# The beginning of a transformer block on one core: zero matmuls, order of the condition rows, and weight splits rearranged

## What is computed

```
emb = silu(t) @ ada_w + ada_b                        # six rows of 512 for each of 4 batches
shift_msa, scale_msa, gate_msa, shift_mlp, scale_mlp, gate_mlp = split(emb, 6)
norm  = ln(x) * (1 + scale_msa) + shift_msa
h     = gelu(norm @ ssm_w1 + ssm_b1)
x     = x + gate_msa * (h @ ssm_w2 + ssm_b2)
norm2 = ln(x) * (1 + scale_mlp) + shift_mlp
hf    = gelu_tanh(norm2 @ ff_w1 + ff_b1)
x     = x + gate_mlp * (hf @ ff_w2 + ff_b2)
# second block: gamma * ln(x) + beta with gamma = w @ Wg.T + bg, beta = w @ Wb.T + bb,
# then qkv, softmax attention over 16 heads, projection, and the same style norm again
```

## Time and profile before

| | |
|---|---|
| median of 3 runs | 1886.05 us (1886.03 to 1886.64) |
| the profiled execution | 1888.92 us |
| its span in the profile | 1887.1 us |
| PE, DVE, ACT, POOL busy | 1817.0, 1249.5, 778.2, 1181.6 us |
| mean granted TensorE clock | 0.987 |

### The profile page before, as it was taken

One profiled execution on the slowest core, in us unless ns is written; L12 is line 12 of the kernel. 1 busy time (PEld: TensorE's weight loads), 2 busy tenths in 40 slices (PEclk: granted clock), 3 DMA queues, 4 the chain that ended last, 5 costly groups with the idle time before them and its releaser, 6 DMA issues. The chain is left out here.

```text
span 1887.1 us, 26913 instructions
## 1 busy us (share of the span) xinstructions
PE 1817.0 (96%) x9530; PEld 1215.4 (64%) x9530; DVE 1249.5 (66%) x2053; ACT 778.2 (41%) x1376; POOL 1181.6 (63%) x655
## 2 busy tenths in 40 slices
PE   7899999999998999999899999999999999999995
PEld 3588888888887788888555555545555554454584
DVE  4565555655655454546787777777777777787399
ACT  2223123222222222221476666666666666666200
POOL 2675465466454212111588888888898888898455
PEclk9999999999999999999899999999999999999998
DMA  7310110100103555474777778778787877765894
GB/s 249 128 41 23 56 34 22 56 33 22 56 1 134 184 188 191 156 244 142 188 164 174 179 182 183 175 171 187 177 183 175 184 175 177 172 150 138 261 400 145
DMA packets 131013, 278.46 MB, mean 148 GB/s; under 512 B 23846, under 2 KB 41382, under 8 KB 122840
## 3 DMA queue, kind: packets, MB, share of 16 engines
q1 hardware_dynamic: 98772, 191.71, 33.6%
q0 software_dynamic: 9264, 66.11, 17.2%
q10 hardware_dynamic: 22872, 19.28, 3.2%
HBM read 134.42 MB, written 75.80 MB: 111 GB/s over the span
## 5 line engine op out<-in xcount | busy, mean ns | idle before, releaser
L1558 DVE TENSOR_REDUCE at_mrow<-banks 128x1 f32<-128x512 f32 x976 | 593.7, 679 | 169.7 <-PE banks L1404 169.6
L1654 POOL TENSOR_TENSOR at_sums<-at_probs 128x2048 f32<-128x2048 f32 x127 | 599.0, 4716 | 94.5 <-DMA at_sums<-at_sums 80.6
L1538 ACT ACTIVATE at_probs<-banks 128x512 f32<-128x512 f32 x1024 | 519.0, 621 | 185.6 <-PE banks L1422 180.5
L1404 PE MATMUL banks<-early_ks,early_qs 96*128 96x512 f32 x976 | 406.7, 417 | 9.8 <-DVE at_mrow L1558 5.4
L1422 PE MATMUL banks<-early_qs,early_ks 98*128 98x512 f32 x1024 | 408.4, 418 | 2.3 <-ACT at_probs L1538 1.8
L1404 PEld LDWEIGHTS banks<-early_ks,early_qs 96*128 96x128 f32 x976 | 184.8, 189 | 141.8 <-DVE at_mrow L1558 87.7
L1422 PEld LDWEIGHTS banks<-early_qs,early_ks 98*128 98x128 f32 x1024 | 193.9, 190 | 107.8 <-ACT at_probs L1538 83.3
L1434 PE MATMUL banks<-at_probs,at_v 128*32 128x512 f32 x2048 | 250.4, 606 | 1.6 <-DMA at_v<-v_scratch 1.6
L71 PE MATMUL banks<-l_ht,l_weights 128*128 128x512 f32 x768 | 179.4, 393 | 7.0 <-ACT l_gt L657 7.0
L71 PE MATMUL banks<-qk_nt,l_weights 128*128 128x512 f32 x768 | 179.8, 392 | 3.0 <-ACT qk_gt L1039 3.0
L71 PE MATMUL banks<-l_weights,l_hf 128*128 128x512 f32 x768 | 177.3, 390 | 0.0
(11 more groups left out here) (143 smaller groups left out, 2100.6 us busy)
## 6 DMA issues: line engine op xcount, KB each, us to landing
at_sums<-at_sums POOLq DMA_DIRECT2D x63, 1024.0 KB, 8.3
qk_scratch<-qk_out SPq DMA_DIRECT2D x64, 512.0 KB, 2.8
early_ks<-qk_scratch SPq DMA_DIRECT2D x48, 512.0 KB, 4.9
early_qs<-qk_scratch SPq DMA_DIRECT2D x96, 256.0 KB, 5.6
attn_scratch<-at_out SPq DMA_DIRECT2D x32, 512.0 KB, 7.6
o_a<-attn_scratch SPq DMA_DIRECT2D x32, 512.0 KB, 12.9
chunk_in<-x SPq DMA_DIRECT2D x8, 1024.0 KB, 5.2
v_scratch<-qk_v ACTq DMA_DIRECT2D x32, 256.0 KB, 2.4
```

The source lines that it names most:

```text
L1404: pe.matmul(em[n % 3][:], qs[0:96, slot, half, j, c * P:(c + 1) * P], ks[0:96, slot, j, keys * CH:(keys + 1) * CH], start=True, stop=True) ...
L1538: nc.scalar.activation(probs[:, i % 4, j, :], et[n % 3][:], ACT.Exp).then_inc(exp_done, 1)
L1558: nc.vector.tensor_reduce(mrow[:, half, keys, u:u + 1], em[n % 3][:], AX.X, ALU.max).then_inc(max_done, 1)
L1654: nc.gpsimd.tensor_tensor(into, probs[:, a], probs[:, a + 1], ALU.add).then_inc(pair_ready, 1)
```

## The change

- In setup PE runs 12 matmuls on two zeroed tiles before its first row. DVE writes the ones into `ones2` only after them (`warmed`).
- PE multiplies the row `GATE_MSA` before it turns the first two rows, not after.
- The copy and the split of weight 1 leave setup: ACT and DVE do them at the start of step 0.
- ACT copies weights 2 and 3 after the second and third tile of L1, and 4 and 5 after the tiles of `U_T2`. DVE splits 2 and 3 between the L1 tiles and 4 after the tiles of `U_T1`; POOL splits 5 after all eight tiles of `U_F1`. PE waits for the last two before its loop, as it did.
- SP issues the loads of weights 2 and 3 ahead of the late rows.
- PE computes two late rows before `turn_ln2` and the third after it. DVE adds their biases in two parts and takes the statistics of the next chunk after the second tile of `U_T2`, not before the first.
- POOL takes the inverse deviation of the next chunk between the second and third of those tiles.

```diff
@@ setup_stage @@
-            act.wait_ge(raw_loaded[1], 16)
-            nc.scalar.copy(sh.w0[:, HI, 1, :], sh.w0_raw[:, LO, 1, :]).then_inc(w_hi, 1)
...
+            pe.wait_ge(dve_step, 2)
+            for _ in range(WARM):
+                ins = pe.matmul(ps[7][:], sh.ones2[:], sh.bias_rows[:], start=True, stop=True)
+            ins.then_inc(warmed, 1)
             pe.wait_ge(silu_ready, 1)
             row(SHIFT_MSA)
             row(SCALE_MSA)
+            row(GATE_MSA)
             pe.wait_ge(consts_loaded, 6 * 16)
             turn_rows(0, 2)
-            row(GATE_MSA)
...
             dve.wait_ge(dve_step, 2)
+            dve.wait_ge(warmed, 1)
             nc.vector.memset(sh.ones2[0:2].bitcast(F32), 1.0)
...
             take_turned(1)
-            low_weight(1)
...
-            pool.wait_ge(w_lo, 2)
+            pool.wait_ge(w_lo, 1)
@@ l0_stage, SP @@
             load_gate(0, 0)
+            for n in range(2, 4):
+                load_weight(n)
             load_late_rows()
-            for n in range(2, 6):
-
-                sp.dma_start(raw_weight(sh, weights, n), weights[n]).then_inc(ff_loaded[n - 2], 16)
+            for n in range(4, 6):
+                load_weight(n)
@@ l0_stage, PE @@
                 if first:
-                    late_rows()
+                    late_rows(range(2))
                     turn_ln2()
+                    late_rows(range(2, 3))
...
-                    pe.wait_ge(ff1_lo, 2)
+                    pe.wait_ge(ff1_lo, 3)
...
-            pe.wait_ge(ff2_lo, 2)
+            pe.wait_ge(ff1_lo, 4)
+            pe.wait_ge(ff2_lo, 1)
@@ l0_stage, ACT @@
+                def high_feed_forward(n):
+                    if n in (1, 2):
+                        high_weight(n + 1, ff_loaded[n - 1])
+
+                if first:
+                    high_weight(1, sh.w2_loaded)
+                gelu(ACT.Gelu, l1_done, s, U_L1, range(KT), C_B1, lo, high_feed_forward if first else None)
                 affine(1, s, (s, U_T2), b, hi)
+                if first:
+                    for n in range(4, 6):
+                        high_weight(n, ff_loaded[n - 2])
@@ l0_stage, DVE @@
+                if first:
+                    hi_parts(uses(s, U_T2), KT, ht, next_stats)
+                    add_late_bias(range(2, 3))
...
+                if first:
+                    dve.wait_ge(ff_hi, 4)
+                    split_in_place(nc.vector, sh, 4).then_inc(ff1_lo, 1)
                 hi_parts(uses(s, U_F1 - (KT if last else 0)), FT, hf)
@@ l0_stage, POOL @@
                 add_gated_bias(0, s, b, x)
-                if first:
-                    split_ff2(4)
...
-                if first:
-                    split_ff2(5)
-                if first:
                     lo_parts(uses(s, U_F1), KT, hf)
                     pool.wait_ge(late_stored, 16 * 4)
                     lo_parts(uses(s, U_F1) + KT, KT, hf[:, :, KT:])
+                    split_ff2(5)
```

More of the change, by code:

```diff
@@ L189, in setup_stage @@
         mod_w_loaded = [sem(f"su_mod_w_loaded{i}") for i in range(NROWS)]
-        raw_loaded = [sem(f"su_raw_loaded{i}") for i in range(2)]
+        raw_loaded = [sem("su_raw_loaded"), sh.w2_loaded]
         silu_ready = sem("su_silu_ready")
@@ L585, in step, with late_rows @@
                     to_features(w1, nt, KT, [m], [a[m]], l1_done)
+                if first:
+                    pe.wait_ge(ff1_lo, 1)
                 to_tokens(w2, ht, KT, b, uses(s, U_L1), l2_done)
-                def late_rows():
+                def late_rows(which):
                     pe.wait_ge(gt_full, uses(s, U_L1) + KT)
-                    for n, row in enumerate(LATE_ROWS):
+                    for n in which:
+                        row = LATE_ROWS[n]
                         pe.wait_ge(late_loaded, 16 * 8)
@@ L667, in gelu, with high_weight @@
                                          bias=sh.cols[:, col + m:col + m + 1]).then_inc(gt_full, 1)
+                    if behind is not None:
+                        behind(n)
             def step(s, parity, b, b_next, last):
                 lo, hi = banks(parity, 0), banks(parity, 1)
[L671 to L676, removed]
+                first = isinstance(s, int) and s == 0
+                def high_weight(n, loaded):
+                    act.wait_ge(loaded, 16)
+                    nc.scalar.copy(sh.w0[:, HI, n, :], sh.w0_raw[:, LO, n, :]).then_inc(ff_hi, 1)
+                def high_feed_forward(n):
[4 more added lines that the diff above has]
+                gelu(ACT.Gelu, l1_done, s, U_L1, range(KT), C_B1, lo, high_feed_forward if first else None)
                 affine(1, s, (s, U_T2), b, hi)
+                if first:
+                    for n in range(4, 6):
+                        high_weight(n, ff_loaded[n - 2])
                 if not last:
@@ L698, in hi_parts @@
                     nc.vector.tensor_copy(dst[:, HI, i, :], gt[:, i % 2, :]).then_inc(gt_hi, 1)
+                    if behind is not None:
+                        behind(i)
             def ln_stats(which, s, src):
@@ L745, in step, with add_late_bias, next_stats @@
                 ln_apply(1, s, x1[:, parity])
[L746 to L749, removed]
-                if first:
+                def add_late_bias(which):
                     dve.wait_ge(late_loaded, 16 * 8)
-                    for n in range(len(LATE_ROWS)):
+                    for n in which:
                         dve.wait_ge(late_ps_ready, n + 1)
                         nc.vector.tensor_tensor(rows[:, n], lo[n][0:B, :], rows[:, n], ALU.add).then_inc(late_ready, 1)
+                def next_stats(i):
+                    if i == 1:
+                        add_late_bias(range(2))
+                        dve.wait_ge(x_loaded, 16 * (s + 1))
+                        ln_stats(0, s + 1, x)
+                if first:
+                    hi_parts(uses(s, U_T2), KT, ht, next_stats)
+                    add_late_bias(range(2, 3))
+                else:
+                    if not last:
+                        dve.wait_ge(x_loaded, 16 * (s + 1))
+                        ln_stats(0, s + 1, x)
+                    hi_parts(uses(s, U_T2), KT, ht)
                 if not last:
@@ L828, in step @@
                 add_gated_bias(0, s, b, x)
[L829 to L831 removed]
+                if not first:
                     add_gated_bias(1, s - 1, b_prev, x1[:, 1 - parity])
                 inv_std(1, s)
[L834 removed]
+                if first:
+                    lo_parts(uses(s, U_T2), KT // 2, ht)
                     inv_std(0, s + 1)
[L836 removed]
+                    lo_parts(uses(s, U_T2) + KT // 2, KT // 2, ht[:, :, KT // 2:])
+                else:
+                    if not last:
+                        inv_std(0, s + 1)
+                    lo_parts(uses(s, U_T2), KT, ht)
                 if first:
```

27 lines of the change are left out of this document (17 added, 10 removed).

## The result

| | before | changed |
|---|---|---|
| median of 15 runs | 1886.64 us | 1892.98 us |
| lowest and highest | 1883.39, 1889.71 | 1888.53, 1897.75 |
| span of the profiled execution | 1887.1 us | 1890.2 us |
| its time | 1888.92 us | 1892.00 us |

The medians lie 6.3 us apart. The ratio of the two sets of runs is 1.0035, with a 95% interval of 1.0028 to 1.0043, which is 5.3 to 8.1 us slower. (More runs of the kernel before were made beside the changed one; the table ahead of the prediction has the first three.)

What follows compares the result with a forecast made beforehand. PE, busy in all but 4%, bounds the kernel, so L1 of chunk 1's start decides: 7.4 us later, plus 2.3 low clock, less a 0.6 wait, +9.0 on 1886.05 gives 1895.0 us; range 1888.5 to 1899.

Steps and rivals of the forecast that it cites:

- Setup: Before step 0: turning at 19.95 us, 2.1 later, yet the stage gives 1.9 and L1 starts at 33.65.
- L1 of step 0: First half of step 0: with no long wait ahead, L1 takes 11.04 us in place of 12.74.
- Weights 2 and 3: First half of step 0: loads without 3 MB ahead land at 43.5 and 46.1 us; L2 ends at 59.0.
- Engines that take turns: DVE splits and POOL tiles exclude each other at two places; without exclusion the sum is 2.4 us less.
- PE at the end of F1: Second half of step 0: PE done with F1 at 96.9 us, before 105.19, so 8.3 us won on PE.
- The low clock behind the new wait: L1 of chunk 1: low clock after PE's 15.7 us wait costs 2.3 us more, between 1.7 and 3.4.
- POOL's tail: POOL's work from the U_T1 tiles to the weight 5 split: 86.4 us plus 26.1, ending at 112.5; PE waits for it.
- The 0.6 ahead of L2: L2 of chunk 1: PE's 0.6 us wait for POOL goes, since POOL is free.
- a change of more than 1 us there: Sign of being wrong: anything behind L1 of chunk 1 changes length by more than 1 us.
- POOL's tail is not last: Faster rival at the loop's branch: POOL ends ahead of PE, PE's 8.3 us stay won, 1877 us; chance 0.08.
- The ends nearly meet: Rival: early loads and no engine exclusion, POOL ends at 107.8, sum +3.8 or less, 1888 to 1889.8 us; chance 0.12.
- The zero matmuls do not lift the clock: Rival in setup: first two rows end at 16.95 as before, turning 0.5 later, total +9.5, 1895.5 us; chance 0.12.

Runs made afterwards that it cites:

- experiment 7: Changed kernel without the 12 zero matmuls and DVE's wait for them; 1893.50 us in one run.
- 1: Changed kernel with POOL's split of weight 5 back ahead of the eight U_F1 tiles; 1884.38 us, ratio 0.9987.
- 2: Changed kernel with PE's wait for the splits of weights 4 and 5 moved from the loop's branch to the second feed-forward product; 1884.14 us, ratio 0.9982.
- 3: On top of 2, the split of weight 5 moved from POOL to DVE, behind its eight U_F1 tiles; 1879.18 us, ratio 0.9956.
- 6: On top of 3, the late rows' four small products moved from POOL to DVE and their stores to SP's queue; 1875.81 us, ratio 0.9940.
- 4: Changed kernel with 56 matmuls on PE in its long wait after F1 of step 0; 1892.76 us, ratio 1.0031.
- 8: Changed kernel with the row GATE_MSA back behind the first turning; 1893.26 us in one run.
- 10: On 6, SP's loads in the old order, late rows ahead of weights 2 and 3; 1885.78 us, ratio 0.9989.
- 9: On 6, the same edit as 5, late rows together; 1879.72 us, ratio 0.9962.
- 5: Changed kernel with late rows, chunk 1 statistics and POOL's inverse deviation in the old order; 1893.99 us, ratio 1.0031.

## Why the prediction was right

The sign, the place, the releaser and the length of the new wait came as forecast. The size was +9.0 (its terms, 7.4 + 2.3 - 0.6, make 9.1) and came out as +6.3 by the medians and +7.4 in the trace, at the start of L2 of chunk 1, within the range.

- **Setup.** The turning stood at 20.06 (19.95 forecast), L1 of step 0 at 33.63 (33.65). Right.
- **L1 of step 0** was to run at full clock, 11.04 us. It took 12.73, with the clock at 0.52 from 33.4 to 36.8:

```profile
33.40:36.80 3.40, 3.17 (x8) 2.53 (x9) 1.49 (x2) 3.18 (x2) 0.00 (x0) 0.52 0.36 98
```

  The step failed: I had taken the waits of 1.42 and 1.12 ahead of it for too short to lower the clock. It cost nothing, since the weight ended last there. In experiment 7 L1 took 11.16 us, and PE then waited 1.78 us in L2 in place of 0.22 (3.3 forecast): the second half began at 51.96 against 52.02.
- **Weights 2 and 3.** This is the term of the sum that was mis-sized. ACT's copy was to start at 43.5 and started at 42.23, 1.3 sooner, inside the bound of 2.3. The second half of L2 began at 52.02 (53.5), L2 ended at 57.65 (59.0), the turning at 66.5 (67.9), F1 began at 72.00 (73.3).
- **Engines that take turns.** POOL's tile beside DVE's second split (46.78, 2.29 us) took 3.33 us, the one beside the split of weight 4 (89.69, 2.28 us) took 3.27, alone 1.29. The choice that these engines exclude each other was right at both places, each worth 2 us for the tile:

```profile
46.88 3.33 POOL L834 TENSOR_TENSOR l_ht<-l_gt,l_ht 128x512 fp32r<-128x512 f32 x1 [3.40 <-DVE l_ht L724]
50.58 1.29 POOL L834 TENSOR_TENSOR l_ht<-l_gt,l_ht 128x512 fp32r<-128x512 f32 x1 [0.36 <-DVE l_ht L724]
```

  The rule of the Trainium skill (SBUF — State Buffer, SBUF: two separate sides), that such operations hold a shared port pair one after the other, agrees with these rows.
- **PE at the end of F1**: 96.9 forecast, 96.9 measured, and that they agree is luck. It should have been 1.3 sooner by the term above, but DVE's normalising of chunk 1 took 4.75 us with POOL at work, in place of 1.9, which the forecast had not priced, and PE's turning took 2.8 us from start to start in place of 1.7, with 0.74 of waiting for it (the products of F1 took some tenths more as well).
- **The low clock behind the new wait** (granted 0.50 from 111 to 115 us) cost 13.16 - 11.04 = 2.1 (2.3).
- **POOL's tail.** The late rows' finish began at 77.64 (79.0) and took 7.63 (7.4), the tail from 85.27 to the split's end 25.4 (26.1). L1 of chunk 1: 111.25 (112.6). The wait: 14.3 (15.7). The 0.6 ahead of L2 is gone, as forecast.
- **Trace to median.** +7.4 is still +7.3 behind the first block, where PE's next turning starts at 613.04 us before and at 620.32 with the change. Behind that point the spans give 1274.1 us before and 1269.9 with the change. The prediction had named a change of more than 1 us there as a sign that it was wrong; since unchanged code varies by more than that from one execution to the next (last section), the sign tells nothing. The medians give +6.3, with an interval of 5.3 to 8.1 that holds it. Between 9.0 and 7.4 stand the weight's landing, 1.3, and small terms that no run here takes apart.

**The rivals.** "POOL's tail is not last" fell for the change as it stands; experiments 1 to 3 and 6 show that the 8.3 us behind it were real, and paid out as soon as PE no longer met POOL's tail: 1877 was its time, and 6 gave 1875.81. That these are so close is partly luck, since 6 also shortens DVE's normalising, which the rival did not count. "The ends nearly meet" had the load right in direction, but not the exclusion. "The zero matmuls do not lift the clock" fell by the 7.03 us for 16 products. The rival of the experiments, that the clock is the loss, is worth 2.0 us (4).

**What was lost where**, in starts of L2 of chunk 1: moving the wait to its reader brings back 11.0 us (124.25 to 113.29), splitting weight 5 on DVE 3.2 more (110.06), and taking the late rows' finish from POOL another 3.2 (106.84), or 1.9 had the clock fallen in F1 as it did in 3. With all three the stretch ends 10 us sooner than before.

## What to carry to other kernels

A wait at the head of a loop stands for all that is queued ahead of it on the releasing engine, so a step that is put into that queue "where there is room" can hold up an engine that doesn't need it: put the wait where the data are read, and follow each engine to the point where they meet before you count a gain. A gain on one engine's path counts only as far as that engine is last there: the same reordering was worth 1.1 us in one version and 4.5 in another (of which 1.7 is the clock), and the warming nothing. When work is moved forward, move its loads forward with it.

## What the runs showed of the hardware that was not expected

- **The clock falls behind short waits too, and not each time.** It fell behind 2.52 us (8), and behind 1.42 and 1.12 with 0.65 of small transposes between in the changed kernel, but not behind the same two in 7, whose L1 took 11.16. Ahead of F1 of step 0 PE waits 1.9 us in nine traces: its first 24 products took 5.7 us in the changed kernel, 1, 4, 6 and 8, and 7.3 in 2, 3, 7 and 10, where the granted clock in the first 3 us was 0.52 to 0.66. No run here shows what decides it. Where PE is last, as in 6, 9 and 10, this moves a start by some 1.5 us from one execution to the next; where PE then waits for POOL, it moves nothing.
- **DVE's normalising takes longer beside POOL's products.** The four tiles of chunk 1 took 4.75 us in the changed kernel, where they stand beside two of POOL's tiles, the first issue of the late rows and the first products, 3.78 in 6, where POOL has only the tiles, and 1.89 in the kernel before, in 5 (1.90) and in 9. Before, and then with the change:

```profile
82.05 1.89 DVE L716 TENSOR_SCALAR l_nt_raw<-chunk_in,l_mv 128x512 f32<-128x512 f32 x4
```

```profile
75.11 4.75 DVE L744 TENSOR_SCALAR l_nt_raw<-chunk_in,l_mv 128x512 f32<-128x512 f32 x4 [0.39 <-POOL l_mv L842]
```

- **POOL's first DMA issue and DVE's normalising: one of the two is long.** The first of the late rows' stores falls beside the normalising in three kernels. It took 0.60 us in the changed kernel, where the normalising took 4.75, and 1.62 before and 1.63 in 5, where the normalising took 1.9. What decides which one gives way no run here takes apart.
- **The rest of the program is not constant.** Behind the first block, whose work no experiment changed, the profiled executions took between 1267.2 us (9) and 1276.5 (5). Before took 1274.1 and the changed kernel 1269.9, so that their spans differ by only 3.1 us where the stretch that was changed differs by 7.3. Single spans cannot resolve this change; starts at the end of the changed stretch can, and so can medians of 10 and more runs, if the difference is several us.
